# Second layer's two weight products in fp16 high and low parts, with the weights scaled and split during the first layer

## The reference, cut to what matters

```python
def _L1_gnn_ref(x, edge_index, eps, W1, b1, g1, be1, W2, b2, g2, be2):
    agg = jax.ops.segment_sum(x[src], dst, num_segments=N)
    h = (1.0 + eps) * x + agg                               # 1250 x 512
    h = jax.nn.relu(batch_norm(h @ W1 + b1, g1, be1))       # 1250 x 1024
    h = h @ W2 + b2                                         # 1250 x 512
    h = jax.nn.relu(batch_norm(h, g2, be2))
    return x + h

h = jnp.maximum(_layernorm(x, axis=-1), 0.0)
x = x + _L0_gnn_ref(h, batch0, edge_index, ...)             # first layer
h = jnp.maximum(_layernorm(x, axis=-1), 0.0)
x = x + _L1_gnn_ref(h, edge_index, ...)                     # second layer
```

## Time and profile before

| | |
|---|---|
| median of 3 runs | 378.61 us (377.73 to 378.73) |
| the profiled execution's own time | 377.62 us |
| span of its trace | 375.7 us |
| TensorE clock granted, mean over the span | 0.999 |
| matmuls in stages Z and U | 576, all in fp32r |
| bytes read from HBM | 14.88 MB |

### The profile page before, as it was taken

The page is one execution under the profiler, slowest core; times in us unless marked ns, Lnnn a source line. Parts: engine busy times, 40 slices in busy tenths (PEclk is TensorE's granted clock), DMA queues, the critical chain, the costliest instruction groups (busy, mean ns, idle before and its releaser), DMA issues.

```text
span 375.7 us, 6123 instructions
## 1 busy us (share of the span) xinstructions
PE 362.1 (96%) x2054; PEld 275.1 (73%) x2054; DVE 238.5 (63%) x644; ACT 174.5 (46%) x303; POOL 97.8 (26%) x159
## 2 busy tenths in 40 slices
PE   8999999989999999999989998999999999999994
PEld 4786656767767666676556654559999999999993
DVE  5889999987876977528977877222354445422324
ACT  1547648779586236120075875212644543423032
POOL 8232120000000000000135879621557462201100
PEclk9999999999999999999999999999999999999999
DMA  6990300000000000005900022100000004020223
GB/s 172 297 287 3 115 2 3 3 3 3 1 3 3 3 3 3 3 2 147 235 6 3 5 107 71 47 2 0 0 2 1 2 0 112 2 55 15 68 54 82
DMA packets 16642, 18.03 MB, mean 48 GB/s; under 512 B 1871, under 2 KB 11023, under 8 KB 16595
## 3 DMA queue, kind: packets, MB, share of 16 engines
q1 hardware_dynamic: 15642, 17.21, 16.4%
q10 hardware_dynamic: 953, 0.23, 0.3%
HBM read 14.88 MB, written 2.56 MB: 46 GB/s over the span
## 4 chain that ended last, share of the span: by engine, by line
PE 69%; DVE 16%; ACT 6%; issue 4%; POOL 2%; DVEq 2%; DMA 0%; SPq 0%; ACTq 0%; POOLq 0%
PE bank L1333 66%; DVE ring L943 2%; DVE st_row L893 1%; DVE hl L1203 1%; ACT hn L672 1%; POOL ln_s L479 1%; DVE w_lo L1222 1%; POOL x L520 1%; PE bank L1715 1%; DVE st_row L1214 1%; DVE x L1211 1%; PE bank L1541 1%; DVE kmax L959 1%; ACT hh L777 1%; DVEq L1063 1%
## 5 line engine op out<-in xcount | busy, mean ns | idle before, releaser
L1333 PE MATMUL bank<-AT,hh 125*128 125x400 f16 (+1 forms) x240 | 80.9, 339 | 2.7 <-DVE hl L1203 2.6
L1333 PE MATMUL bank<-AT,hl 125*128 125x400 f16 (+1 forms) x240 | 80.7, 338 | 0.0
L488 POOL TENSOR_TENSOR bn_tmp<-var_eps,minus_half 128x1 f32<-128x1 f32 (+1 forms) x15 | 9.6, 642 | 183.9 <-DVE var_eps L1035 183.8
L943 DVE TENSOR_SCALAR ring<-iota_code,code 125x250 f16<-125x250 f16 x200 | 46.2, 307 | 1.9 <-issue 1.8
L1333 PEld LDWEIGHTS bank<-AT,hh 125*128 125x128 f16 x240 | 23.2, 97 | 21.7 <-DVE hl L1203 3.3
L1333 PEld LDWEIGHTS bank<-AT,hl 125*128 125x128 f16 x240 | 23.4, 97 | 18.0 <-issue 0.2
L1333 PE MATMUL bank<-a_hi,w_hi 128*128 128x400 f32 (+1 forms) x96 | 34.2, 356 | 0.0
L1333 PE MATMUL bank<-agg_hi,w_hi 128*128 128x400 f32 (+1 forms) x96 | 34.0, 355 | 0.0
L1333 PE MATMUL bank<-a_hi,w_lo 128*128 128x400 f32 (+1 forms) x96 | 33.8, 352 | 0.0
L1333 PE MATMUL bank<-agg_hi,w_lo 128*128 128x400 f32 (+1 forms) x96 | 33.8, 352 | 0.0
L1333 PE MATMUL bank<-agg_lo,w_hi 128*128 128x400 f32 (+1 forms) x96 | 33.8, 352 | 0.0
(11 more groups left out here) (215 smaller groups left out, 742.7 us busy)
## 6 DMA issues: line engine op xcount, KB each, us to landing
x_in<-x SPq DMA_DIRECT2D x5, 448.0 KB
x<-x SPq DMA_DIRECT2D x2, 1120.0 KB
w_s<-w SPq DMA_DIRECT2D x2, 1024.0 KB, 10.1
w_s<-w SPq DMA_DIRECT2D x4, 512.0 KB, 4.4
out<-x SPq DMA_DIRECT2D x6, 224.0 KB
wB<-wk SPq DMA_DIRECT2D x1, 1024.0 KB, 9.3
wA<-wq SPq DMA_DIRECT2D x1, 1024.0 KB, 13.4
wC<-w_conv SPq DMA_DIRECT2D x1, 1024.0 KB, 15.2
```

The source lines that it names most:

```text
L488: own.step(pool.tensor_tensor(bn_tmp[:, 1, k:k + n], var_eps[:, k:k + n], minus_half[:, 0:n], ALU.pow))
L943: return dve.tensor_scalar(ring[:, slot, j, a:b], iota_code[0:CH, a:b], code[:, bass.ds(c + j, 1)], float(-CODES * t), ALU.subtract, ALU.i ...
L1333: return pe.matmul(o, l, r, start=start, stop=stop, skip_group_check=True)
```

## The change

- `agg_hi`, `agg_lo`, `a_hi`, `a_lo` and the high and low parts of W1 and W2 become fp16. The matmuls are the same in number, order and shape.
- W1 and W2 are multiplied by 1/sqrt(mean square) before they are split, the aggregate by 1/(32 max(1, |1 + eps|)), and this is undone by a scale in the copies out of PSUM (`undo_w`) and in the last block's statistics.
- W1 is loaded in the first layer into two buffers of its own; its sums of squares stand in slots 20 and 21 on ScalarE, the sum over partitions is piece `F1` in slot 22 on TensorE, the high parts stand in slots 23 and 24, the low parts on VectorE after O3 and after slot 24. The uses of W1 in the row loop are gone.
- W2 is loaded in two halves of 1 MB when the last window is counted. Squares, mean and high parts stand on ScalarE after slot 25, piece `F2` on TensorE between A31 and D2, the low parts on VectorE at b = 1 and b = 2 of stage Z. All other uses of it are gone.
- SyncE's load of x1 now also waits for W1's low parts (`s_w1l`).
- The terms of eps are made after slot 24 on VectorE (five small steps), the undo terms (five more) after the row loop; the small step on eps behind A32 is gone.
- Many buffers get new places.

```diff
 SLOTS: ... "QT3 A30"  ->  "QT3 A30 F1"
-LAST = "A31 D2 A02 A12 A22 A32".split()
+LAST = "A31 F2 D2 A02 A12 A22 A32".split()
-W1_AT = (3, 7)
+SQ1_AT, HIGH1_AT = (20, 21), (23, 24)
...
-        agg_hi = place("agg_hi", [P, FB, N], F32R, 88)
-        agg_lo = place("agg_lo", [P, FB, N], F32R, 107.5625)
+        agg_hi = place("agg_hi", [P, FB, N], F16, 88)
+        agg_lo = place("agg_lo", [P, FB, N], F16, 97.78125)
...
-        w1_hi = place("w1_hi", [P, FB, HID], F32R, 138)
-        w1_s = place("w1_s", [P, 2, HID], F32, 190)
-        a_hi = place("a_hi", [P, HB, N], F32R, 8)
+        w1_s = [place(f"w1_s{half}", [P, 2, HID], F32, at) for half, at in enumerate((92, 162))]
+        w1_hi = place("w1_hi", [P, FB, HID], F16, 138)
+        w2_s = [place(f"w2_s{half}", [P, HB // 2, D], F32, at) for half, at in enumerate((112.75, 120.75))]
+        a_hi = place("a_hi", [P, HB, N], F16, 8)
+        a_lo = place("a_lo", [P, HB, N], F16, 45)
...
 SyncE
+            sp.wait_ge(full[PLACE["V1"][0]], PLACE["V1"][1] + 1)
+            sp.dma_start(w1_s[1][:], w_t(w1)[:, 2:4, :]).then_inc(sem("d_w11"), 16)
+            sp.wait_ge(sem("s_wcl"), 1)
+            sp.wait_ge(full[PLACE["G0"][0]], PLACE["G0"][1] + 1)
+            sp.dma_start(w1_s[0][:], w_t(w1)[:, 0:2, :]).then_inc(sem("d_w10"), 16)
+            sp.wait_ge(sem("s_win"), NW)
+            for half in range(2):
+                sp.dma_start(w2_s[half][:], w_t(w2)[:, 4 * half:4 * half + 4, :]).then_inc(sem(f"d_w2{half}"), 16)
             sp.wait_ge(full[PLACE["WO1"][0]], PLACE["WO1"][1] + 1)
+            sp.wait_ge(sem("s_w1l"), 2)
...
 GpSimd
+            for layer in range(2):
+                pool.wait_ge(sem(f"s_mean_w{layer}"), 1)
+                m, s = mean_w[layer], scale_w[layer]
+                own.step(pool.tensor_scalar(m[:, 1:2], m[:, 0:1], 1e-30, None, ALU.add))
+                pool.tensor_tensor(s[:, 0:1], m[:, 1:2], minus_half[:, 0:1], ALU.pow).then_inc(sem(f"s_scale_w{layer}"), 1)
...
-                pool.tensor_tensor(a_lo[:, b, :], zr[:, b % 2, :], a_hi[:, b, :].bitcast(F32), ALU.subtract)\
+                pool.tensor_tensor(a_lo[:, b, :], zr[:, b % 2, :], a_hi[:, b, :], ALU.subtract)\
                     .then_inc(sem("s_al"), 1)
...
 ScalarE
+            def weight_squares(layer, half):
+                raw_w, junk = ((w1_s, sq1), (w2_s, sq2))[layer]
+                act.wait_ge(sem(f"d_w{layer + 1}{half}"), 16)
+                if half:
+                    act.wait_ge(sem(f"s_ssq_w{layer}"), half)
+                act.activation(junk[:], raw_w[half][:], ACT.Square, accum_out=ssq_w[layer][:, half:half + 1])\
+                   .then_inc(sem(f"s_ssq_w{layer}"), 1)
+            def weight_high(layer, half):
+                act.wait_ge(sem(f"s_scale_w{layer}"), 1)
+                hi, raw_w = ((w1_hi[:, 2 * half:2 * half + 2, :], w1_s), (w2_hi[:, 4 * half:4 * half + 4, :], w2_s))[layer]
+                act.activation(hi, raw_w[half][:], ACT.Identity, scale=scale_w[layer][:, 0:1])\
+                   .then_inc(sem(f"s_w{layer + 1}h"), 1)
...
+                if t in SQ1_AT:
+                    weight_squares(0, SQ1_AT.index(t))
+                if t in HIGH1_AT:
+                    weight_high(0, HIGH1_AT.index(t))
                 for name in SLOTS[t]:
                     if late(name):
                         attention(name)
+            act.wait_ge(sem("s_win"), NW)
+            act.wait_ge(full[PLACE["O3"][0]], PLACE["O3"][1] + 1)
+            for half in range(2):
+                weight_squares(1, half)
+            weight_mean(1)
+            for half in range(2):
+                weight_high(1, half)
...
-                if i in W1_AT:
-                    half = W1_AT.index(i)
-                    act.wait_ge(sem("d_w1"), 16 * (half + 1))
-                    copy(w1_hi[:, 2 * half:2 * half + 2, :], w1_s[:]).then_inc(sem("s_w1h"), 1)
...
 VectorE
+            def weight_low(layer, half):
+                dve.wait_ge(sem(f"s_w{layer + 1}h"), half + 1)
+                ...
+                dve.scalar_tensor_tensor(lo[:, ks, :], raw_w[half][:], scale_w[layer][:, 0:1], hi[:, ks, :],
+                                         ALU.mult, ALU.subtract).then_inc(sem(f"s_w{layer + 1}l"), 1)
...
                 for name in SLOTS[t]:
                     piece(name)
+                    if name == "O3":
+                        weight_low(0, 0)
             low_counts(NW - 1)
+            weight_low(0, 1)
+            aggregate_terms()
...
-                if i - 2 in W1_AT:
-                    half = W1_AT.index(i - 2)
-                    dve.wait_ge(sem("s_w1h"), half + 1)
-                    dve.tensor_tensor(w1_lo[:, 2 * half:2 * half + 2, :], w1_s[:], ...)
             low_rows(T - 1)
+            undo_terms()
...
-                if b == 3:
-                    w2_low(0)
+                if b in (1, 2):
+                    weight_low(1, b - 1)
...
 TensorE
+                if name in ("F1", "F2"):
+                    layer = int(name[1]) - 1
+                    pe.wait_ge(sem(f"s_ssq_w{layer}"), 2)
+                    ps = open_group(pe, name)[:, 0:1]
+                    for half in range(2):
+                        ins = mm(ps, ssq_w[layer][:, half:half + 1].broadcast_to([P, P]), ones32[:], half == 0, half == 1)
+                    close_group(ins, name)
+                    return
```

136 lines of the change are left out of this document (72 added, 64 removed), and 4 rows, old and new, of tables (LONE_BANKS, SLOTS).

## The result

The changed kernel takes 367.87 us (367.83 to 368.03, 4 runs), against 378.56 us (377.73 to 378.73) for the kernel before on the same chip: ratio 0.9728, 95% interval 0.9715 to 0.9741. The profiled execution took 367.88 us, and its span is 366.0 us. The forecast was 369.7 for the median, with 367.0 to 374.0 as its range, and 368.7 for the profiled execution.

The account below looks back on a forecast made before the run. TensorE, busy 96%, was taken to bound the kernel, with VectorE setting the row loop's end. Removing 8.3 and 3.3 us and adding 1.2 and 1.5 left 8.9 us gained: 369.7 us, range 367.0 to 374.0.

Parts of the forecast that it names:

- Z and U: Stages Z and U: blocks of 36 matmuls go from 6.86 to 6.34 us with fp16, removing 8.3 us.
- Row loop: Row loop: without W1's steps on VectorE, tiles stay 2.99 us apart and aggregation starts at 227.3, removing 3.3 us.
- The undo steps: After the row loop: five VectorE steps fit before the first B group closes, costing nothing, below 1 us if shown.
- F1 and F2: First layer, TensorE: four fp32 matmuls on the path add 1.2 us, bounds 0.4 and 2 us.
- FR's hold-up: First layer: piece FR, with one fp32 matmul, held the weight path 0.30 us, taken as each matmul's price.
- The cover of F2: Before D2: W2's square ends at 172.6, F2's turn comes about 175.5, so 3 us of cover and no cost.
- the lag: VectorE, first layer: about 1.2 us reaches A21 and is gone at WO0; costed at nothing, up to 2 us.
- The Z chain: GpSimd's a_lo chain in Z makes TensorE wait about 1.5 us in block 7 of U's first f.
- rival (a): Z chain stays hidden, as GpSimd is delayed less or fp16 is quicker for it: 368.2 us, chance 0.17.
- The remaining aggregation and the tail: From the row loop's end to Z, and after U's last matmul: forecast to change by 0 us.
- From the profiled execution to the median: Whole kernel: median forecast at 369.7 us, profiled execution at 368.7, so 1.0 us between them.
- the wait of 1.5 us: Stage U: TensorE enters at 50.8, wants block 7's last low part at 63.0, gets it at 64.5.

Follow-up runs that it names:

- types_only: The kernel before with only the eight operands of the second layer's products made fp16, no scaling and the weights handled at their old places: 370.37 us.
- loop_low: The changed kernel with VectorE writing the first half of W1's low part again after tiles 5 and 9 of the row loop: 372.08 us.
- adds_late: The changed kernel with GpSimd's last three additions to x1 moved from the row loop's end to behind the aggregate's sixth low part: 367.39 us.
- undo_moved: The changed kernel with VectorE's five small undo steps moved from the row loop's end to behind the fifth step on the aggregate: 368.81 us.
- f_four: The changed kernel with the two fp32 matmuls of F1 and of F2 issued four times over, twelve more in all: 370.38 us.
- z_low_four: The changed kernel with two more of VectorE's low parts of W2 in stage Z, at b = 3 and 4: 371.73 us.
- a_lo_long: The changed kernel with an unused GpSimd subtraction of 125 columns ahead of each a_lo: 370.20 us.
- small_costs: The changed kernel with four unused GpSimd subtractions of differing types after the last a_lo, and a constant scale in two stage Z blocks' copies: 377.94 us (one run).
- low_early: The changed kernel with W2's two low parts on VectorE moved from stage Z to behind the sixth and seventh aggregate steps: 367.86 us.

## Why the prediction was right, and where not

- **Z and U, -8.3 forecast, -8.26 measured.** The price of a matmul was taken from fp16 rows of the same widths in another stage, and it held to a hundredth; that those have 125 partitions did not matter. `types_only` shows it by itself. Why fp32r is slower wasn't tried. By the Trainium skill, "TensorE: Matmul & The Clock Gate", "Weight-path perf modes — Fast Weight Load (FWL) and DoubleRow", the faster way of loading weights is open to types other than FP32; of fp32r that section of the Trainium skill says nothing. The halved busy time of the weight loads agrees.
- **Row loop, -3.3 forecast, -2.47 measured.** That W1's low parts on VectorE made the loop long was right (`loop_low`: +3.09); that they did so by filling VectorE's own list was right at most in part, since at tile 9 of `loop_low` TensorE waits through GpSimd's small step. And the size was off. The step that failed is "From a tile's transposes to the end of its low half it took 208.16 + 0.69 - 202.60 = 6.25 us for tile 3, so tile 9's low half ends at 226.8". It ended at 228.07. Half of that is no error of this step, as all of the loop begins 0.69 us later by F1 and F2; from tile 9's transposes (221.22) it took 6.85 us and not 6.25. Tile 9's low half isn't tile 3's: by then GpSimd runs its three last additions back to back. The row that says so is in the earlier trace rows: 1.76 us for the last low half of the kernel before (there too GpSimd's three additions run beside it, from 226.24 on), against 0.69 for tile 3's, and I took its end from it without asking for its length. The 0.64 us by which it is too long and half of the 0.31-us wait behind it come back when the additions move (`adds_late`: 0.76). With the undo steps below, this is the whole 0.8 us that is missing.
- **The undo steps, 0 forecast.** They do show, by 0.25 us (`undo_moved`), inside the loop's number: I had said they fit before the first B group closes, and had costed them alone, without GpSimd beside them.
- **F1 and F2, +1.2 forecast, +0.69 measured.** FR's hold-up of 0.30 us was a weight load's duration; a fp32 matmul of one column costs 0.19 to 0.22 us in a row of them (`f_four`). The two pieces waited for nothing: F1 at 145.30 and F2 at 175.68 have no gap ahead. The cover of F2 was 4.2 us where I had 3, and on VectorE the lag reached A21 and was gone by WO0, as forecast; it had 0.55 us of idle time left there and 0.96 before A32.
- **The Z chain, +1.5 forecast, nothing measured: rival (a).** The two low parts each cost a_lo 2.05 us (I had the whole 2.35), the chain did run at GpSimd's own pace, and it surfaces at the place named once it is longer (`z_low_four`, `a_lo_long`). By the prediction the last low part of block 7 ends 64.5 us after Z's start and is wanted at 63.0. Measured from Z's start (252.34) it is wanted at 62.94, so that half was right, and it ends at 61.30, 3.2 us early. The terms: a_lo in fp16 takes 2.56 us, not 2.90, 7 x 0.34 = 2.4 us, since the value of fp32r was carried over to a type that no row showed; the two low parts cost 0.3 us less each; and the way from the last a_lo to that low part takes 4.98 us, not 5.2. That leaves 1.6 us of cover, near the 1.59 that both runs show. With a_lo at 2.90 the wait would have been 2.4 - 1.59 = 0.8 us by these numbers, an estimate, not 1.5; with the a_lo that fp16 has, the low parts at their full 2.35 us would still have been covered.
- **The remaining aggregation and the tail, +0.14 and +0.2, 0 forecast.** Not tested. In the tail two VectorE steps on the last block's statistics read one more scale than before and take 0.21 and 0.26 us where they took 0.15 and 0.20, ahead of those the output waits for. That is 0.1 of the 0.2 us, and only read from the rows.
- **From the profiled execution to the median, +1.0 forecast, nothing measured.** The prediction put the 1.0 us by which the median of the kernel before lay above its profiled execution onto the changed kernel too. The changed kernel's median and profiled execution are 367.87 and 367.88. This is the larger part of the 1.8 us between 369.7 and 367.87.

The errors (0.8 us too much gain in the loop and 0.3 of small costs unseen; 0.5 and 1.5 too much cost in F1, F2 and the chain) offset one another in part, and the sum was 0.8 us off: 8.9 forecast, 9.7 in the span. That it came so near is in part luck: the wait of 1.5 us, the forecast's third largest term, didn't come at all, and rival (a), at 368.2, is nearer in time and right on the chain.

The Trainium skill's page "SBUF — State Buffer", "SBUF: two separate sides", holds that whichever of the two engines starts first has the shared ports for its whole instruction. Three runs agree: 2.46 us for a 0.43-us subtraction beside a low part, 1.33 for a 0.69-us low half beside the additions (the changed kernel against `adds_late`), and VectorE's pieces at the length of GpSimd's subtractions in `small_costs`.
The 2.6 cycles for each element that the Trainium skill gives in "GPSIMD Engine Reference", "Elementwise — side-by-side cycle accounting", were measured for an addition in fp32; that they hold "whatever else", as the prediction has it, the Trainium skill doesn't say. Here a subtraction with fp32 inputs and result takes 2.82 us, near the estimate of 2.7 by it, and one with an fp16 input and an fp16 result 2.56; for fp16 the measurement decides.

## What to carry to other kernels

Price a matmul by the distance between starts, in rows of the new type and the same width, wherever in the trace they stand. Before taking a duration from a loop's middle for its end, look at the last iteration's own row: what the other engines pile up there is not what they do in the middle. When a chain is set against TensorE, ask which piece of the operand each matmul waits for; and when work is moved into an engine's idle time, ask what shares its port there, not only whether its list is empty.

## What the hardware showed that I had not expected

- Right behind a wait of 3.87 us TensorE ran at half clock (0.65, then 0.50, back by 184 us), and the first tile of the row loop came 5.87 us late. Nothing in the expectation had a place for that. The traces have three more such falls to 0.50: in or behind waits of 2.75 us (`low_early`), 2.77 us (`a_lo_long`) and 5.00 us (`small_costs`), at a price of 1.8, 1.2 and 2.2 us beyond the wait. Behind waits of 1.92 us (`loop_low`) and 1.43 us (`z_low_four`) the clock stayed at 1.00. A cover that fails can cost more than its shortfall.
- GpSimd's subtraction of 1250 columns takes 2.56 us if the second input and the result are both fp16, and 2.81 to 2.85 with one or none of them; types did matter.
- VectorE's conversion of 400 columns to fp16, a step with a single input, took 2.71 us beside GpSimd's subtractions and 0.36 alone: it, too, waits for the port. A small two-input step on one column took 0.97 us on VectorE beside the additions and 0.16 without them, and GpSimd's `ln_b` 1.83 us beside a low part and 0.19 without.
- ScalarE's copy out of PSUM costs 0.09 us more when its scale is read per partition (673 against 578 ns for 400 columns). By the Trainium skill, "ScalarE: Activation LUTs", "What ACT_TABLE_LOAD costs", each such operand adds about 93 ns; the trace agrees.
